# Row scatters spaced over steps, and expert tiles' result scatters issued in pairs, in a two-layer graph and mixture-of-experts kernel on one core

## What is computed

```python
x = x + gnn0(layernorm(x), adj, h0, y)      # adj masked by y @ y.T, rows divided by their l1 sum, 0.9 * support + 0.1 * h0
x = x + ffn0(layernorm(x), ...)             # shared expert (512 hidden) + the best 2 of 8 experts (512 hidden each)
x = x + gnn1(layernorm(x), adj, adj, W, b)  # [x, adj @ x, rowsum(adj * adj.T)] @ W + b
x = x + ffn1(layernorm(x), ...)             # the best 2 of 8 experts (256 hidden each)
```

## Time and profile before

| | us |
|---|---|
| three timed executions | 1468.39, 1472.78, 1475.87 |
| their median | 1472.78 |
| span of the profiled execution | 1555.4 |
| of that TensorE busy (matmul) | 1367.5 (88%) |
| VectorE busy | 929.2 (60%) |
| ScalarE busy | 649.6 (42%) |
| GpSimd busy | 461.5 (30%) |

### The profile page before, as it was taken

The page is one execution under the profiler, slowest core; times in us unless marked ns, Lnnn a source line. Parts: engine busy times, 40 slices in busy tenths (PEclk is TensorE's granted clock), DMA queues, the critical chain, the costliest instruction groups (busy, mean ns, idle before and its releaser), DMA issues.

```text
span 1555.4 us, 21717 instructions
## 1 busy us (share of the span) xinstructions
PE 1367.5 (88%) x6536; PEld 829.7 (53%) x6536; DVE 929.2 (60%) x2670; ACT 649.6 (42%) x1108; POOL 461.5 (30%) x450
## 2 busy tenths in 40 slices
PE   5998999999999999998689999999999998766771
PEld 2443444444444444456578877466666666545550
DVE  6775858576776767684322224777777777432224
ACT  3454344343444433444244344565555555422220
POOL 2102021111202020213545554223323332465652
PEclk9999999999999999999899999999999999978885
DMA  9688988696888787875366442889888888433435
GB/s 314 253 335 315 337 297 305 239 341 238 321 274 317 265 318 266 304 248 206 104 250 223 170 165 96 312 296 311 296 292 308 304 287 250 117 111 113 126 109 202
DMA packets 117360, 386.22 MB, mean 248 GB/s; under 512 B 20116, under 2 KB 49587, under 8 KB 87824
## 3 DMA queue, kind: packets, MB, share of 16 engines
q1 hardware_dynamic: 77296, 327.32, 60.9%
q10 hardware_dynamic: 27136, 33.93, 6.2%
q0 software_dynamic: 12832, 23.81, 4.3%
HBM read 332.80 MB, written 57.41 MB: 251 GB/s over the span
## 4 chain that ended last, share of the span: by engine, by line
PE 51%; issue 12%; DVE 10%; another core or an unknown queue 5%; ACT 4%; POOL 3%; DMA 2%; DVEq 0%; POOLq 0%; ACTq 0%; SPq 0%
PE agg L742 14%; PE d L846 7%; PE s L726 6%; PE d L790 4%; POOL rows_scratch L1798 3%; PE d L800 2%; PE d L680 2%; DVE adj_over_wb L386 2%; PE agg L913 2%; PE u L831 2%; PE u L833 2%; ACT h L1101 2%; PE u L827 1%; PE u L832 1%
## 5 line engine op out<-in xcount | busy, mean ns | idle before, releaser
L742 PE MATMUL agg<-m,xn 128*128 128x512 f32 (+1 forms) x800 | 399.4, 585 | 0.0
L1065 ACT ACTIVATE mabs<-m 128x512 f32<-128x512 f32 (+1 forms) x400 | 243.7, 619 | 322.4 <-DVE m L1561 289.4
L1561 DVE TENSOR_TENSOR m<-s,ring 128x512 f32<-128x512 f32 (+1 forms) x400 | 268.2, 676 | 184.2 <-PE s L726 127.7
L726 PE MATMUL s<-ymov,ysta 128*128 128x512 f32 (+1 forms) x400 | 244.8, 616 | 42.7 <-DVE m L1561 24.7
L1798 POOL DMA_INDIRECT rows_scratch<-xrow,idx x160 | 183.8, 1149 | 297.8 <-DVE xrow L1306 102.8
L1807 POOL DMA_INDIRECT y_scratch<-yo,ids x164 | 160.9, 981 | 138.9 <-DVE yo L1456 70.8
L742 PEld LDWEIGHTS agg<-m,xn 128*128 128x128 f32 x800 | 152.2, 191 | 62.8 <-issue 41.9
L726 PEld LDWEIGHTS s<-ymov,ysta 128*128 128x128 f32 x400 | 75.3, 190 | 199.7 <-issue 97.8
L386 DVE TENSOR_TENSOR adj_over_wb<-ring,adj_over_wb 128x512 fp32r<-128x512 f32 (+1 forms) x216 | 138.8, 672 | 48.5 <-ACT adj_over_wb L1165 44.7
L1784 POOL TENSOR_TENSOR rstd<-vareps,mhalf 128x4 f32<-128x4 f32 x30 | 38.3, 1277 | 405.6 <-DVE vareps L1218 405.6
L1165 ACT CAST adj_over_wb<-ring 128x512 fp32r<-128x512 f32 (+1 forms) x216 | 125.6, 607 | 45.7 <-PE agg L920 42.6
(11 more groups left out here) (242 smaller groups left out, 1982.8 us busy)
## 6 DMA issues: line engine op xcount, KB each, us to landing
ring<-in_adj_in SPq DMA_DIRECT2D x180, 1024.0 KB
ring<-in_adj_out SPq DMA_DIRECT2D x30, 1024.0 KB
wb<-blob_scratch SPq DMA_DIRECT2D x27, 834.0 KB
rows_scratch<-yo ACTq DMA_DIRECT2D x81, 260.0 KB, 6.7
stage<-in_adj_out SPq DMA_DIRECT2D x19, 1024.0 KB
ring<-in_adj_in SPq DMA_DIRECT2D x20, 784.0 KB
xt<-rows_scratch SPq DMA_DIRECT2D x54, 260.0 KB
wbz<-blob_scratch SPq DMA_DIRECT2D x27, 193.0 KB
```

The lines of the kernel that those rows point to most:

```text
L726: pe.matmul(sbank[s % 2][:, 0:n], ysta[:, s * P:(s + 1) * P], ymov[:, k % 2, 0:n], start=True, stop=True).then_inc(s_made, 1)
L742: pe.matmul(abank[:, 0:n], xn[:, b, :], m[:, b % M_BUFS, 0:n], start=b == 0, stop=b == NB - 1).then_inc(S["agg_blocks"], 1)
L1065: act.activation(mabs[:, b % ABS_BUFS, 0:width(k)], m[:, b % M_BUFS, 0:width(k)], ACT.Abs).then_inc(abs_made, 1)
L1561: dve.tensor_tensor(m[:, s % M_BUFS, 0:width(k)], sbank[s % 2][:, 0:width(k)], slot_part(LOAD_AT[k, l, False][0], s % LB, width(k)), ALU.m ...
```

## The change

Three things change in GpSimd's program; the other engines' programs stay as they are. In the first loop, for all iterations but the last, a group's first six row scatters stand in steps 29, 31, ... 39, each behind a wait for that many finished blocks of the iteration (`m_made`), and its last two in steps 1 and 3 of the next iteration. In the second loop the first three stand in steps 36, 38 and 40, the other five in steps 1, 3, 5, 7 and 9 of the next iteration, each behind a wait for finished blocks (`agg_blocks`); in the last iteration they stand in the same steps without these waits. After the loops, the four scatters of a tile are issued as two and two, the later two behind a wait for two down steps of the next tile.

```diff
+A_SPREAD = ((29, 31, 33, 35, 37, 39), (1, 3))
+Z_SPREAD = ((36, 38, 40), (1, 3, 5, 7, 9))
...
-        def scatter_tile(t):
+        def scatter_pair(t, half):
 
             layer, buf = tile_layer(t), yo_buf(t)
-            pool.wait_ge(yo_made, t + 1)
-            for q in range(TB):
+            if half == 0:
+                pool.wait_ge(yo_made, t + 1)
+            for q in (2 * half, 2 * half + 1):
                 pool.indirect_dma_start(
...
+        def scatter_tile(t):
+
+            scatter_pair(t, 0)
+            scatter_pair(t, 1)
+
+        def run_tiles(layer, first):
+
+            last = (layer + 1) * TILES
+            for t in range(first, last):
+                scatter_pair(t, 0)
+                if BESIDE[layer] <= t % TILES + 1 < TILES:
+                    pool.wait_ge(tile_down, hidden_before(t + 1) + 2)
+                scatter_pair(t, 1)
...
-                if mid and A_AT["scatter"] <= s < A_AT["scatter"] + 2 * TB:
+                if k == CH and A_AT["scatter"] <= s < A_AT["scatter"] + 2 * TB:
                     scatter_rows(0, k - 1, s - A_AT["scatter"])
+                if mid and k < CH and s in A_SPREAD[0]:
+                    pool.wait_ge(m_made, k * NB + s)
+                    scatter_rows(0, k - 1, A_SPREAD[0].index(s))
+                if k >= 2 and s in A_SPREAD[1]:
+                    if k < CH:
+                        pool.wait_ge(m_made, k * NB + s)
+                    scatter_rows(0, k - 2, len(A_SPREAD[0]) + A_SPREAD[1].index(s))
...
-        for t in range(2, TILES):
-            scatter_tile(t)
+        run_tiles(0, 2)
...
-                if mid and s == at["scatter"]:
+                last = isinstance(k, int) and k == CH
+                if last and s == at["scatter"]:
                     for i in range(2 * TB):
                         scatter_rows(1, CH + k - 1, i)
+                if mid and not last and s in Z_SPREAD[0]:
+                    wait(pool, SZ["agg_blocks"], k * NB + s - LAG)
+                    carry(pool, pool_carried)
+                    scatter_rows(1, CH + k - 1, Z_SPREAD[0].index(s))
+                if s in Z_SPREAD[1] and not (isinstance(k, int) and k < 2):
+                    if not last:
+                        wait(pool, SZ["agg_blocks"], k * NB + s)
+                        carry(pool, pool_carried)
+                    scatter_rows(1, CH + k - 2, len(Z_SPREAD[0]) + Z_SPREAD[1].index(s))
...
-        for t in range(TILES + 4, 2 * TILES):
-            scatter_tile(t)
+        run_tiles(1, TILES + 4)
```

## The result

The changed kernel takes 1480.97 us (median of 6 executions, 1478.26 to 1485.93), the kernel before 1472.32 us (median of 6, 1468.39 to 1475.87). The ratio is 1.0068 with a 95% interval of 1.0052 to 1.0085: 8 to 13 us slower, where the forecast was 10 us faster. It is near the time that rival 1 gave, about 1480. The profiled execution of the changed kernel has a span of 1483.7 us and its own device time was 1485.93, so this profile, unlike the one of before, is of an execution as long as the plain ones.

A forecast was written before the change was run, and what follows sets the result against it. Prediction: both loops bound by TensorE products, neither TensorE nor GpSimd full in the second layer's tiles. Terms -7 -2 +8 -10 +1 = -10 us on the profiled 1555.4, carried over unchanged to 1472.8, gave 1463 us; range 1444 to 1488.

The forecast's parts named there:

- rival 1: Whole kernel: unnamed waits belong to the profiled execution, so -7 and -10 vanish and the late norm stays; about 1480 us, chance 0.28.
- There neither is full: Second layer's expert tiles: of 200 us TensorE is busy 134 and GpSimd 119, so neither engine is full.
- First loop, -7: First loop: spacing row scatters wins back unnamed VectorE waits inside their runs; 7 us gained, between nothing and 11.
- as the run ends: First loop: a 3.82 us unnamed VectorE wait ends at 279.86, when the run of eight row scatters ends.
- Second loop, -2: Second loop: spaced scatters land before the normalization is ready; gain 2.5 us, 2 taken; with slow landing a further loss of 7.
- T0: Second loop: start of the iteration's first block, 1078.50 us in the first profile; other times count from it.
- neither 3.4 nor 7.1 us: Second loop: two readings of the last scatter's landing time, 3.4 us after four close scatters, 7.1 after a run with a 3.75 us scatter.
- rival 2: Second loop: last scatter, tied to the ninth block, lands late every iteration, so the norm waits; price 7 us, total 1489, chance 0.17.
- Tiles and tail, -10 and +1: Second layer's tiles: pairs shorten the 12.9 us two-tile pattern towards 10.2, 10 us gained; delayed second pair at the end costs 1.
- the 82.6 us: Whole kernel: the median of plain runs, 1472.78 us, lies this far below the profiled span of 1555.4.
- Late last group, +8: Second loop's last iteration: scatters queued behind power and first tile delay the norm 10 to 14 us; cost 2 to 13, taken 8.
- Rival 3: Whole kernel: scatter runs cost through shared transfer engines only, spreading returns nothing, idle time absorbs the late group; 1473 us, chance 0.15.

The follow-up runs named there:

- the second profile: The kernel before, unchanged, profiled once more: time 1470.93 us, profile span 1468.8 us, where the first profile had 1555.4.

## Why the prediction was wrong

**What bounds the kernel.** For the two loops the reading stood: TensorE is busy 667 of 703 and 303 of 320 us in the changed kernel's profile too, and GpSimd's new order changed neither loop by an amount that can be seen. For the second layer's tiles it failed. "There neither is full" was a busy share over an execution with 59.2 us of unnamed waits and took the 0.3 us between scatters for free time. In an undisturbed execution GpSimd issues 108 tile and eight row scatters there without a pause, and 1.03 us more for it a tile was about as much more for the kernel.

**First loop, -7.** Measured 0 to +4. The step that failed is the choice between the two ends: that the waits end "as the run ends" I took for cause. With the same runs of scatters, the second profile has nothing over 0.74 us inside them, where I had summed 17.2 us, so the low end that I named (nothing, if they come from something else) was right.

**Second loop, -2.** Measured -2 to +3. The sum took the spacing to move nothing in itself, with the last scatter started at T0+7.8 to 8.2. It starts at T0+9.3 in six of the changed kernel's eight iterations, 1.3 us later than before. The last scatter's landing was the right question, but neither 3.4 nor 7.1 us belongs to a spacing, and 3.4 was not a landing: the norm of the earlier trace rows stands at T0+14.0, just where it stands when only the power holds it (T0+13.95), so that row gives only an upper bound. Where the norm does stand late, in both profiles of before and in the one with the second loop spaced alone, it stands 4.7 to 7.2 us after that scatter's start. The mechanism that I saw in the earlier trace rows, an iteration about 1 us longer when the norm waits long, is real: with the second loop spaced alone, norm waits of 1.77 and 1.38 us stand in iterations that last 37.2 and 37.1 us from power to power, against 36.0 to 36.3 in the second profile of before, where the same two waits are 0.47 and 0.66 us. How often it strikes isn't set by the change in any way that these profiles show: in the changed kernel one norm of eight is late, by 0.7 us, where rival 2 had all of them late. The prediction's own check, all scatters near 1 us, failed too. The changed kernel in one iteration of the second loop:

```profile
1034.34 0.49 PE L922 MATMUL agg<-adj_over_wb,ysta 128*128 128x512 f32 x1 [0.76 <-ACT aggf L1173]
...
1036.11 0.96 POOL L1802 DMA_INDIRECT rows_scratch<-xrow,idx  x1 [2.18 <-PE agg L924]
1037.51 2.82 POOL L1802 DMA_INDIRECT rows_scratch<-xrow,idx  x1 [0.44 <-issue]
...
1040.64 1.43 POOL L1802 DMA_INDIRECT rows_scratch<-xrow,idx  x1 [0.30 <-issue]
...
1043.63 0.96 POOL L1802 DMA_INDIRECT rows_scratch<-xrow,idx  x1 [0.30 <-issue]
```

The long scatter, 3.75 us in the earlier trace rows, is 2.82 us here. It starts at T0+3.2 instead of T0+2.2, and ends at T0+6.0 in both. So it ends at one place of the iteration whether or not the scatters before it are spaced out, and isn't a matter of their number in a row; what holds it is not shown. The three after it are bunched by it, and the spacing wanted is lost.

**Tiles and tail, -10 and +1.** Measured -1 to +2 for the pairs as a whole. The 12.9 us pattern of the earlier trace rows was the disturbed execution. In the second profile of before, two tiles after the loop take 10.3 to 11.0 us from first scatter to first scatter, eight scatters back to back with a few longer ones among them: the floor of 10.2 that I wrote down as the best the change could reach, or close to it. There was nothing left to gain. The checks that I had named for a right forecast, this pattern under 12 us and no long unnamed wait in the first loop, are both met by the changed kernel, but the kernel before meets them too. The prediction had the number and the sentence ("GpSimd will soon run gapless again"), and didn't ask whether it ran gapless already in the timed executions, which the 82.6 us should have raised.

**Late last group, +8.** Mechanism and sign right: 8 to 14 us measured alone. By the parts: the eighth scatter starts 7.75 us after the power's start, as worked out (1350.7 less 1343.07 is 7.6); it let the norm go 2.35 us later, less than the 3.4 to 7.1 that I took, so the norm is 8.9 us late and not 10 to 14 (it stands 10.1 us after the power's start; I had 10.9 to 15). But GpSimd ends up 11.3 us late and not 7 to 10: I counted only its wait for the second tile, and the third and fourth added 3.55 and 2.18 us. And nothing absorbed any of it, because the "unnamed idle time" that was to do so is in none of the undisturbed profiles. The landing taken too long and the waits left out go opposite ways: at the second tile GpSimd is 6.0 us late, less than the 7 to 10, and only the next two tiles bring it to 11.3. That +8 came near is in part luck. From the start of that power to the last scatter of all the changed kernel takes 164.43 us (1294.06 to 1458.49), the second profile of before 152.77 (1291.08 to 1443.85): +11.7 us, which is within the 8 to 13 us of the result. The profile of the changed kernel is another 3 us behind at that power (1294.06 against 1291.08), but it was 2.8 us behind already at VectorE's first product of the first loop (16.68 against 13.84), ahead of any row scatter, so that isn't the change.

**Sum.** The single step that turned the sign is the last one, "carried over unchanged". A sum that contains -7 and -10 of waits without a named cause, from an execution 82.6 us longer than the plain ones, is not a sum about the plain ones. Rival 1 had it right in what it is about, the unnamed waits gone and the late norm left; its sum, 8 + 1 - 2 = 7 us slower, is a little under the 8 to 13 measured, with a late norm priced some 3 us short and two small terms of which nothing was seen. I gave it 0.28 because the waits "end with the scatters' run each time", a coincidence in time that I ranked above the 82.6 us. Rival 3, that spreading returns nothing, was right for the loops, but the idle time that was to absorb the late last group wasn't there. The sentence about what would show the forecast wrong ("the profile shrinks and the plain times don't") is what happened. The range, 1444 to 1488, holds the result; the direction was wrong.

On the page of the Trainium skill that the prediction weighed, "DMA: Bandwidth & Descriptors", section "Anatomy of one DMA": the estimate of 2.2 us that follows from it for a 66,560-byte scatter is nearly met by the last group's eighth scatter, which let the norm go 2.35 us after its start with no scatter issued behind it. With both scatters right behind the power and the first tile's behind them it took 3.3 us (1296.69 to 1300.02). In the loops, beside the adjacency loads, 7.1 us stood; there the measurement decides.

## What to carry to other kernels

Before a profile is summed up, its span belongs beside the plain times: where it is several per cent longer, waits without a named cause are to be taken as that execution's until a second profile shows them again. Whether an engine is full is told by its gaps, held against the gap that it always leaves between two of its operations, and not by its busy share; here a window with GpSimd 65% busy held a stream of 152 us without a pause. And in a program that every engine walks in order, a step moved to "the same place in the next iteration" has to be followed past the special last iteration, where other work is queued between: two scatters of 1.3 us, one queued behind a power and one behind a tile as well, cost 8 to 14 us, and putting them ahead took all of it away.

## What the runs showed of the hardware

One execution of an unchanged program was 86.6 us longer in the profiler than another (1555.4 against 1468.8), spread over all stages (19, 28, 5 and 35 us), with VectorE idle for no named reason for up to 10.9 us at a time. The ten other profiles of this study have spans within 5.2 us of their kernel's median.

An indirect scatter of 128 rows costs GpSimd 1.27 to 1.29 us from start to start when they follow each other, of which 0.96 to 0.98 us is recorded as busy; the 116 of the second layer's tiles and last group took 151.7 us (1293.14 to 1444.82), a few of them being longer ones, and no busy share shows that in full. A small elementwise operation between two scatters, itself recorded with 1.06 us, adds 1.03 us: it starts without a gap behind one scatter, and the 0.3 us gap before the next shrinks to 0.19 us.
